# A deformable-convolution block: the gathered cells hold bilinear coefficients, made on VectorE, and ScalarE leaves the sampling

## The chip, the core and the metric

The kernel runs on one core of a Trainium2 chip. The metric is the device time of one execution in microseconds (us); before the change the median of three runs is 2737.15 us (2737.09 to 2738.84). TensorE (PE), VectorE (DVE), ScalarE (ACT), GpSimd (POOL) and SyncE (SP) run their own instruction streams and meet at semaphores.

## The reference

The input `x` has 4 images of 128 channels by 80x80 pixels, in float32. In short:

```
out_normal = conv3x3(x, w_normal)
offset     = concat(conv3x3(x, w_offx), conv3x3(x, w_offy))      # 18 channels: dy, dx of 9 taps
out_x, out_y = deform_conv(x, offset, w_dx), deform_conv(x, offset, w_dy)
out = relu(bn1(conv3x3(concat(out_normal, out_x, out_y), w_fusion)))   # 384 -> 128 channels
out = relu(bn2(conv3x3(out, w_conv2)) + x)

# deform_conv: for each pixel and tap (k) the position is (y + ky - 1 + dy, x + kx - 1 + dx),
# y0, x0 = its floors, ty, tx = what is left; outside the image a corner counts as zero:
s = (1-ty)(1-tx) x[y0,x0] + (1-ty)tx x[y0,x0+1] + ty(1-tx) x[y0+1,x0] + ty tx x[y0+1,x0+1]
result = sum over taps and channels of w[:, :, k] * s
```

Both deformable convolutions use the same samples `s`.

## The kernel before

**Tiling.** Each image is cut into 10 strips of 8 rows, 640 pixels, so there are 40 strips (`NS`) and 44 steps (`STEPS`); a step works on several strips at different stages. A strip has 9 taps, and the pixels of a tap are 5 tiles of 128 pixels (`TILES`). So a strip needs 45 gathers (`PER`), each of 128 cells, one per partition. A counter `T` numbers the taps of all strips, 360 in all.

**The cell table.** In device memory lies `cell_table`, one row of 2 KB per padded pixel: the 128 channels of its four neighbours (two of the upper row, two of the lower). SP builds it by DMAs from memory to memory (`fill`, L250 to L255): the first image's part whole, ahead of all else but the first loads, and the others in 27 parts of 768 rows, one per step.

**A tap's samples.** POOL issues an indirect DMA per tile (L318) into one of 15 cell slots; it waits until the slot's last reader is through (`mixed_done`) and until PE has come within five taps (`pace`). ACT then scales the upper pair (`upper`, L525, recorded at L495), DVE adds the lower pair (L700), giving `mixed`; ACT scales the left half (`left`, L533, recorded at L495), DVE adds the right half (L706), giving `samp`, pixels by channels. PE turns the five tiles to channels by pixels (`turn_samples`, L395); ACT copies the result rounded to `samp_hi` (L494), DVE subtracts to get `samp_lo` (L659), and PE multiplies both with the weights of the two deformable convolutions (`deform_tap`, lines L363, L366 and L369 of `three`, three matmuls per product). Between these PE works off slices of the other convolutions, by the table `SLICES`: C (second convolution), O (offsets), F (fusion) and N (normal).

**Order.** Each engine's program is written out in order, tap by tap. In step i, tap k, with T = 9i + k, PE turns the samples of T+1, then does its slices, then the products of T. ACT does `left` of T+2, `samp_hi` of T+1, `upper` of T+3. DVE does both its adds of T+2 (`sample`), then `samp_lo` of T+1. At a strip's end ACT and DVE empty the four accumulators (`feat<-acc`), and DVE works out the offsets' floors, fractions and row numbers (`indices`, L676 to L693). SP's program in a step is: load the strip after next (L248), load the residual (L286), fill a table part (L255), store an output strip after waiting for ACT (L294). The weights come in four chunks, split into a rounded and a remaining part by ACT and DVE (`w_hi` at L494, `w_lo` at L659).

Of the kernel before, what the change touches and what calls it, by code (L numbers as in the profile page):

```python
# [7 lines left out]
F32 = mybir.dt.float32  # L8
# [7 lines left out]
TAPS = 9  # L16
# [17 lines left out]
PART = 768  # L34
PARTS = CELLS // PART
FLAT = B * CELLS + 2 * PART
CELL = 4 * C
# [11 lines left out]
GSLOTS = 15  # L49
PACE_LAG = 5 * TILES  # L50
# [45 lines left out]
class Flags:  # L96


    def __init__(self, i=None, table=True):
# [17 lines left out]
        self.table = table if mid else i < (B - 1) * PARTS  # L117
# [17 lines left out]
def deform_block(nc, x, xflat, xpix, weights, bn, const, out):  # L135
    ctx = ExitStack()
    with ctx:
# [5 lines left out]

        table = nc.dram_tensor("cell_table", (B * CELLS, CELL), F32).ap()

# [35 lines left out]
        mixed = sb("mixed", [128, 2, TILES, 2 * C])  # L181
        samp = sb("samp", [128, 2, TILES, C])
# [20 lines left out]
        first_table, table_part = sem("first_table"), sem("table_part")  # L203
# [4 lines left out]
        slot_taken = sem("slot_taken")  # L208
# [33 lines left out]
        def _(eng):  # L242
# [7 lines left out]
            def fill(first, n, sem_):  # L250

                for row in range(2):
                    src = xpix[bass.ds(first + row * PITCH, n), :]
                    pairs = bass.AP(tensor=src.tensor, offset=src.offset, ap=[[C, n], [1, 2 * C]])
                    eng.dma_start(table[bass.ds(first, n), row * 2 * C:(row + 1) * 2 * C], pairs).then_inc(sem_, 16)  # L255
# [9 lines left out]
            fill(0, CELLS, first_table)  # L265
            load_weights(1)
            load_x(1)

            def step(i, par, fl):
                if isinstance(i, int) and i == 0:  # L270
                    eng.wait_ge(samp_done, PER // 3)
                if fl.load:
                    load_x(i + 2)
                if isinstance(i, int) and i == 1:
                    eng.wait_ge(w_lo_done, 2)
                    load_weights(2)
                    eng.wait_ge(w_lo_done, 3)
                    load_weights(3)
# [20 lines left out]
            eng.wait_ge(table_part, 32 * (B - 1) * PARTS)  # L299
# [4 lines left out]
        @block.gpsimd  # L304
        def _(eng):
            eng.memset(feat[:].bitcast(F32), 0.0).then_inc(zeroed, 1)
            eng.memset(mid[:].bitcast(F32), 0.0).then_inc(zeroed, 1)

            def gather(c, par, b):
                at_least(eng, idx_ready, c + 1)  # L310
                for q in range(PER):
                    k, j, g = q // TILES, q % TILES, q % GSLOTS
                    at_least(eng, mixed_done, PER * c + q - GSLOTS + 1)
                    at_least(eng, pace, PER * c + q - PACE_LAG + 1)
                    if not isinstance(c, int):

                        eng.sem_inc(slot_taken, 1)
                    eng.indirect_dma_start(  # L318
                        out=cells[:, g, :], out_offset=None, in_=table[0:(b + 1) * CELLS, :],
                        in_offset=bass.IndirectOffsetOnAxis(ap=index[:, par, j, k:k + 1], axis=0),  # L320
                    ).then_inc(cells_in[g], 16)


            eng.wait_ge(w_hi_done, 1)
            eng.wait_ge(w_lo_done, 1)
            for b in range(B):

                if b == 0:
                    eng.wait_ge(first_table, 32)
                else:  # L330
                    eng.wait_ge(table_part, 32 * PARTS * b)
                for c in range(b * STRIPS, (b + 1) * STRIPS):
                    gather(c, c % 2, b)
# [5 lines left out]
        def _(eng):  # L339
# [50 lines left out]
            def turn_samples(T, tp):  # L390

                at_least(eng, samp_done, TILES * T + TILES)
                at_least(eng, samp_lo_done, T)
                for j in range(TILES):
                    ins = eng.transpose(turned[:, j * 128:(j + 1) * 128], samp[:, tp, j, :], ident)  # L395
                ins.then_inc(samp_turned, 1)
# [20 lines left out]
            turn_samples(0, 0)  # L417

            def step(i, par, fl):
                early = isinstance(i, int) and i < 4  # L420
                for k in range(TAPS):
# [5 lines left out]
                    if fl.strip and (k < TAPS - 1 or fl.nxt):  # L427
                        turn_samples(T + 1, 1 - tp)
# [62 lines left out]
        def _(eng):  # L491
# [27 lines left out]
            def upper(T, c, k, par, tp):  # L519

                at_least(eng, samp_done, TILES * (T - 1))
                for j in range(TILES):
                    g, n = (k * TILES + j) % GSLOTS, (k * TILES + j) // GSLOTS + 1
                    at_least(eng, cells_in[g], (PER // GSLOTS * 16) * c + 16 * n)
                    copy(mixed[:, tp, j], cells[:, g, 0:2 * C], scale=wgt[:, par, 0, 0, j, k:k + 1])\  # L525
                        .then_inc(upper_done, 1)

            def left(T, k, par, tp):

                at_least(eng, samp_turned, T - 1)  # L530
                for j in range(TILES):
                    at_least(eng, mixed_done, TILES * T + j + 1)
                    copy(samp[:, tp, j], mixed[:, tp, j, 0:C], scale=wgt[:, par, 0, 1, j, k:k + 1]).then_inc(left_done, 1)  # L533
# [19 lines left out]
            upper(0, 0, 0, 0, 0)  # L553
            left(0, 0, 0, 0)
            x_high(1, 1)
            upper(1, 0, 1, 0, 1)
            samples_high(0, 0)
            left(1, 1, 0, 1)
            upper(2, 0, 2, 0, 0)
# [3 lines left out]
            def step(i, par, fl):  # L563
                for k in range(TAPS):
                    T = i * TAPS + k
                    tp = (par + k) % 2
                    if fl.strip and k < TAPS - 2:
                        left(T + 2, k + 2, par, tp)
                    elif fl.strip and fl.nxt:
                        left(T + 2, k + 2 - TAPS, 1 - par, tp)  # L570
# [5 lines left out]
                    if fl.strip and k < TAPS - 3:  # L576
                        upper(T + 3, i, k + 3, par, 1 - tp)
                    elif fl.strip and fl.nxt:
                        upper(T + 3, i + 1, k + 3 - TAPS, 1 - par, 1 - tp)
# [76 lines left out]
        def _(eng):  # L656
# [39 lines left out]
            def sample(T, k, par, tp):  # L696

                for j in range(TILES):
                    at_least(eng, upper_done, TILES * T + j + 1)
                    eng.scalar_tensor_tensor(  # L700
                        out=mixed[:, tp, j], in0=cells[:, (k * TILES + j) % GSLOTS, 2 * C:4 * C],
                        scalar=wgt[:, par, 1, 0, j, k:k + 1], in1=mixed[:, tp, j], op0=ALU.mult, op1=ALU.add,
                    ).then_inc(mixed_done, 1)
                for j in range(TILES):
                    at_least(eng, left_done, TILES * T + j + 1)
                    eng.scalar_tensor_tensor(  # L706
                        out=samp[:, tp, j], in0=mixed[:, tp, j, C:2 * C],
                        scalar=wgt[:, par, 1, 1, j, k:k + 1], in1=samp[:, tp, j], op0=ALU.mult, op1=ALU.add,
                    ).then_inc(samp_done, 1)
# [47 lines left out]
            sample(0, 0, 0, 0)  # L757
            x_low(1, 1)
            sample(1, 1, 0, 1)
            samples_low(0, 0)  # L760

            def step(i, par, fl):
                for k in range(TAPS):
# [3 lines left out]
                    if fl.strip and k < TAPS - 2:  # L767
                        sample(T + 2, k + 2, par, tp)
                    elif fl.strip and fl.nxt:
                        sample(T + 2, k + 2 - TAPS, 1 - par, tp)  # L770
# [95 lines left out]
```

## Time and profile before

| what | before |
|---|---|
| median of 3 runs | 2737.15 us |
| profiled execution: span, which is all that is shown of its time | 2989.8 us |
| PE busy, share of the span | 2685.1 us, 90% |
| ACT busy | 2004.2 us, 67% |
| POOL busy | 1870.2 us, 63% |
| DVE busy | 1849.5 us, 62% |
| bytes moved by DMA | 579.32 MB |
| mean granted TensorE clock | 0.983 |

The profiled execution is 253 us longer than the median of the runs; the profile does not say where these lie. "Busy" adds up the time that an engine's instructions cover. "Idle before" is time in which an engine did nothing ahead of an instruction, put down to what ended last before it; "issue" means that the profile shows nothing that it waited for. PE's matmuls overlap by construction, so a PE that is busy is not PE at its peak.

### The profile page before, as it was taken

To read this page: it belongs to the slowest core of one execution; us is meant where nothing else is said; L and a number is where in the kernel's file an instruction comes from. 1 tells how busy PE (TensorE), PEld (TensorE's weight loads), DVE (VectorE), ACT (ScalarE), POOL (GpSimd) and SP (SyncE) were. 2 spreads that over 40 slices of the span, in tenths; PEclk is the share of its full clock that TensorE was granted. 3 is DMA by queue.
4 is the path that set the end of the run, shared out by engine and by line. 5 is a ranking of instruction groups with operands and counts; after the bars stand their busy time and mean duration, and the time that the engine had idled before them with its cause. 6 is when DMAs were issued, how large, how long until landed. Compare 5 with 4: busy or idle time off the path is not lost.

```text
span 2989.8 us, 51480 instructions
## 1 busy us (share of the span) xinstructions
PE 2685.1 (90%) x17840; PEld 2612.5 (87%) x17840; DVE 1849.5 (62%) x4940; ACT 2004.2 (67%) x4925; POOL 1870.2 (63%) x1806
## 2 busy tenths in 40 slices
PE   1558899998999999999999999999999999999999
PEld 1458889998999998999899999999999999999999
DVE  3566666666666666666666666666666666666640
ACT  2566677776767676777677677776676776767741
POOL 3666666666666666666666666666666666666620
PEclk9789999999999999999999999999999999999999
DMA  9676667666666666666666767766666666666620
GB/s 278 202 231 193 206 200 220 202 208 198 205 205 201 198 208 199 201 206 205 204 204 203 215 209 219 215 181 186 183 186 183 181 182 186 186 182 185 179 90 23
DMA packets 218596, 579.32 MB, mean 194 GB/s; under 512 B 31840, under 2 KB 87264, under 8 KB 217952
## 3 DMA queue, kind: packets, MB, share of 16 engines
q0 software_dynamic: 144000, 471.97, 53.7%
q1 hardware_dynamic: 74336, 104.06, 10.5%
q8 instruction: 141, 2.31, 0.3%
q14 instruction: 119, 0.97, 0.1%
HBM read 562.80 MB, written 69.73 MB: 212 GB/s over the span
## 4 chain that ended last, share of the span: by engine, by line
PE 61%; ACT 13%; DVE 9%; issue 8%; another core or an unknown queue 7%; DMA 2%; POOL 1%; ACTq 0%; SPq 0%; POOLq 0%
PE work L363 13%; PE work L369 13%; PE work L366 13%; ACT mixed L495 5%; PE turned L395 5%; PE acc L369 5%; PE acc L366 5%; PE acc L363 5%; ACT samp L495 3%; DVE mixed L700 3%; PE work L348 2%; DVE feat L659 2%; DMA cell_table<-in_xpix 2%; DVE samp L706 2%
## 5 line engine op out<-in xcount | busy, mean ns | idle before, releaser
L318 POOL DMA_INDIRECT cells<-cell_table,index x1800 | 1859.0, 1033 | 1002.6 <-issue 390.4
L495 ACT ACTIVATE mixed<-cells,wgt 128x256 f32<-128x256 f32 x1800 | 758.0, 498 | 29.7 <-DMA cells<-cell_table,index 20.8
L495 ACT ACTIVATE samp<-mixed,wgt 128x128 f32<-128x128 f32 x1800 | 623.1, 396 | 205.6 <-issue 103.6
L700 DVE SCALAR_TENSOR_TENSOR mixed<-cells,wgt,mixed 128x256 f32<-128x256 f32 x1800 | 744.8, 478 | 21.8 <-ACT mixed L495 16.5
L363 PE MATMUL work<-feat,w_hi 128*128 128x320 f32 x2160 | 694.0, 321 | 13.7 <-issue 10.0
L369 PE MATMUL work<-feat,w_lo 128*128 128x320 f32 x2160 | 678.1, 314 | 10.9 <-issue 10.4
L366 PE MATMUL work<-feat,w_hi 128*128 128x320 f32 x2160 | 677.2, 314 | 7.4 <-issue 7.1
L706 DVE SCALAR_TENSOR_TENSOR samp<-mixed,wgt,samp 128x128 f32<-128x128 f32 x1800 | 512.0, 346 | 62.0 <-ACT samp L495 34.3
L659 DVE TENSOR_TENSOR samp_lo<-turned,samp_hi 128x640 fp32r<-128x640 f32 x360 | 295.8, 822 | 393.0 <-ACT samp_hi L494 329.2
L494 ACT ACTIVATE samp_hi<-turned 128x640 fp32r<-128x640 f32 x360 | 250.9, 697 | 374.3 <-remote 265.1
L363 PE MATMUL acc<-samp_hi,w_hi 128*128 128x320 f32 x1440 | 451.0, 313 | 11.9 <-issue 7.0
L366 PE MATMUL acc<-samp_lo,w_hi 128*128 128x320 f32 x1440 | 449.1, 312 | 12.7 <-issue 12.6
L369 PE MATMUL acc<-samp_hi,w_lo 128*128 128x320 f32 x1440 | 448.8, 312 | 8.5 <-issue 8.4
L363 PEld LDWEIGHTS work<-feat,w_hi 128*128 128x128 f32 x2160 | 409.3, 189 | 21.8 <-issue 21.5
L369 PEld LDWEIGHTS work<-feat,w_lo 128*128 128x128 f32 x2160 | 408.9, 189 | 14.2 <-issue 13.8
L366 PEld LDWEIGHTS work<-feat,w_hi 128*128 128x128 f32 x2160 | 409.5, 190 | 10.1 <-issue 10.1
L395 PE MATMUL turned<-cst,samp 128*128 128x128 f32 x1800 | 268.3, 279 | 165.9 <-DVE samp_lo L659 68.1
L395 PEld LDWEIGHTS turned<-cst,samp 128*128 128x128 f32 x1800 | 217.3, 143 | 190.9 <-issue 153.4
L369 PEld LDWEIGHTS acc<-samp_hi,w_lo 128*128 128x128 f32 x1440 | 273.5, 190 | 16.4 <-issue 16.3
L363 PEld LDWEIGHTS acc<-samp_hi,w_hi 128*128 128x128 f32 x1440 | 274.7, 191 | 13.9 <-DVE feat L659 7.7
L366 PEld LDWEIGHTS acc<-samp_lo,w_hi 128*128 128x128 f32 x1440 | 273.8, 190 | 14.0 <-issue 13.6
L363 PE MATMUL work<-mid,w_hi 128*128 128x320 f32 x720 | 233.5, 324 | 6.6 <-issue 6.5
(70 smaller groups left out, 3199.4 us busy)
## 6 DMA issues: line engine op xcount, KB each, us to landing
cell_table<-in_xpix SPq DMA_DIRECT2D x54, 768.0 KB
cells<-cell_table,index POOLq DMA_INDIRECT x1800
x_raw<-in_xflat SPq DMA_DIRECT2D x40, 410.0 KB
cell_table<-in_xpix SPq DMA_DIRECT2D x2, 6912.0 KB, 38.3
late<-in_x SPq DMA_DIRECT2D x40, 320.0 KB
out<-late SPq DMA_DIRECT2D x40, 320.0 KB
late<-in_weights SPq DMA_DIRECT2D x3, 1152.0 KB, 32.5
cells<-in_weights SPq DMA_DIRECT2D x1, 657.0 KB, 4.1
```

Source lines behind the costliest of these rows:

```text
L318: eng.indirect_dma_start(out=cells[:, g, :], out_offset=None, in_=table[0:(b + 1) * CELLS, :], in_offset=bass.IndirectOffsetOnAxis(ap=inde ...
L348: ins = eng.matmul(work[half][:, 0:HR * PITCH], w_off[:, ky, w].rearrange("p g n -> p (g n)"), part[:, par, rows, :], start=(n == 0), stop ...
L363: ins = eng.matmul(dst, taps_hi[:, w], hi, start=start, stop=False, skip_group_check=True)
L366: ins = eng.matmul(dst, taps_hi[:, w], lo, start=False, stop=False, skip_group_check=True)
L369: return eng.matmul(dst, w_lo[:, w], hi, start=False, stop=stop, skip_group_check=True)
L395: ins = eng.transpose(turned[:, j * 128:(j + 1) * 128], samp[:, tp, j, :], ident)
L494: return eng.activation(dst, src, ACT.Copy)
L495: return eng.activation(dst, src, ACT.Copy, scale=scale)
L659: return eng.tensor_tensor(dst, src, hi.bitcast(F32), ALU.subtract)
L700: eng.scalar_tensor_tensor(out=mixed[:, tp, j], in0=cells[:, (k * TILES + j) % GSLOTS, 2 * C:4 * C], scalar=wgt[:, par, 1, 0, j, k:k + 1], ...
L706: eng.scalar_tensor_tensor(out=samp[:, tp, j], in0=mixed[:, tp, j, C:2 * C], scalar=wgt[:, par, 1, 1, j, k:k + 1], in1=samp[:, tp, j], op0 ...
```

## The change

The host now lays out `corners`, a table of the four neighbours of every padded pixel, in place of the table that was filled on the device. From it 72 parts of 384 rows are loaded to on-chip memory, turned by DVE into coefficients, and stored to `coef_table`: the cell then holds a, b-a, c-a and (d-c)-(b-a). A sample is then (c0 + ty*c2) + tx*(c1 + ty*c3): one multiply-add of 256 wide and one of 128 wide, both on DVE. The first five strips (`RAW`) still gather from `corners` and keep the four operations of before. There are 12 cell slots in place of 15, `mixed` has three buffers in place of two and receives the result of the second operation as well, the pace lag is 6 taps in place of 5, and `samp_done` counts taps in place of tiles. ACT's `upper` runs one tap earlier, DVE's first operation runs a tap ahead of its second. SP stores and loads the parts behind the output's store, and loads the last weight chunk behind them.

```diff
-GSLOTS = 15
-PACE_LAG = 5 * TILES
+GSLOTS = 12
+PACE_LAG = 6 * TILES
+MIXED = 3
+LOT = 3
+PART = 128 * LOT
+RAW = 5
+PARTS_AT = [5, 5, 4, 4] + [4, 4, 4, 3, 3] + 18 * [2]
...
+        n = PARTS_AT[i] if i < len(PARTS_AT) else 0
+        self.parts = {j * TAPS // n: FIRST_PART[i] + j for j in range(n)}
...
+            def load_part(p):
+                at_least(eng, part_out, 16 * p)
+                eng.dma_start(coef[...], part_rows(corners, p)).then_inc(part_in, 16)
+            def store_part(p):
+                at_least(eng, part_done, 2 * p + 2)
+                eng.dma_start(part_rows(table, p), coef[...]).then_inc(part_out, 16)
...
-            fill(0, CELLS, first_table)
             load_weights(1)
             load_x(1)
+            load_part(0)
...
-                if fl.table:
-                    at_least(eng, table_part, 32 * i)
-                    fill(CELLS + i * PART, PART, table_part)
                 if fl.second:
                     s = i - 4
                     at_least(eng, out_ready, 2 * s + 2)
                     eng.dma_start(out[:, bass.ds(s * PIX, PIX)], resid[:, par]).then_inc(out_stored[par], 16)
+                for p in fl.parts.values():
+                    store_part(p)
+                    if p + 1 < B * PARTS:
+                        load_part(p + 1)
+                if isinstance(i, int) and i == 1:
+                    eng.wait_ge(w_lo_done, 3)
+                    load_weights(3)
...
+            for c in range(NS):
+                b = c // STRIPS
+                if c < RAW:
+                    gather(c, c % 2, corners[0:CELLS, :])
+                    continue
+                if c == RAW or c % STRIPS == 0:
+                    eng.wait_ge(part_out, 16 * PARTS * (b + 1))
+                gather(c, c % 2, table[0:(b + 1) * CELLS, :])
...
+            def upper(T):
+                if T >= TAPS * RAW:
+                    return
...
+            def weigh(T):
+                if T >= TAPS * RAW:
+                    return
...
+            def rows_mixed(T):
+                k, par, raw = T % TAPS, T // TAPS % 2, T < TAPS * RAW
+                if not raw:
+                    at_least(eng, samp_turned, T - MIXED + 1)
+                for j in range(TILES):
+                    n = T * TILES + j
+                    cell, into = cells[:, n % GSLOTS, :], mixed[:, T % MIXED, j]
+                    if raw:
+                        at_least(eng, upper_done, n + 1)
+                    else:
+                        at_least(eng, cells_in[n % GSLOTS], 16 * (n // GSLOTS) + 16)
+                    eng.scalar_tensor_tensor(
+                        out=into, in0=cell[:, 2 * C:4 * C], scalar=wgt[:, par, 1, 0, j, k:k + 1],
+                        in1=into if raw else cell[:, 0:2 * C], op0=ALU.mult, op1=ALU.add,
+                    ).then_inc(mixed_done, 1)
+            def sampled(T):
...
+                for j in range(TILES):
+                    ins = eng.scalar_tensor_tensor(
+                        out=mixed[:, buf, j, 0:C], in0=mixed[:, buf, j, C:2 * C],
+                        scalar=wgt[:, par, 1, 1, j, k:k + 1], in1=mixed[:, buf, j, 0:C], op0=ALU.mult, op1=ALU.add)
+                ins.then_inc(samp_done, 1)
+            def coefficients(p):
+                at_least(eng, part_in, 16 * p + 16)
+                eng.tensor_tensor(coef[:, :, :, 1], coef[:, :, :, 1], coef[:, :, :, 0], ALU.subtract).then_inc(part_done, 1)
+                at_least(eng, part_done, 2 * p + 1)
+                eng.tensor_tensor(coef[:, :, 1], coef[:, :, 1], coef[:, :, 0], ALU.subtract).then_inc(part_done, 1)
...
-                    if fl.strip and k < TAPS - 2:
-                        sample(T + 2, k + 2, par, tp)
...
+                    sampled(T + 2)
                     if fl.strip and (k < TAPS - 1 or fl.nxt):
                         samples_low(T + 1, 1 - tp)
+                    rows_mixed(T + 3)
+                    if k in fl.parts:
+                        coefficients(fl.parts[k])
```

## Rows read from the trace of the kernel before

**Rows 1.** Busy time of each engine over the span, from the page.

```profile
PE 2685.1 (90%) x17840; PEld 2612.5 (87%) x17840; DVE 1849.5 (62%) x4940; ACT 2004.2 (67%) x4925; POOL 1870.2 (63%) x1806
```

**Rows 2.** Busy time by stretch: window, length, engines, clock, DMA share, GB/s.

```profile
66.00:132.00 66.00, 32.40 (x182) 31.05 (x181) 41.33 (x113) 41.60 (x107) 46.51 (x46) 0.82 0.68 211
132.00:200.00 68.00, 42.23 (x233) 39.36 (x231) 44.23 (x120) 44.31 (x113) 47.26 (x46) 0.80 0.66 198
500.00:2700.00 2200.00, 2069.95 (x13906) 2018.01 (x13905) 1429.89 (x3832) 1553.10 (x3831) 1443.94 (x1404) 1.00 0.66 198
```

**Rows 3.** Timeline of the first 66 us: start, length, engine, line, [idle before <-releaser].

```profile
2.58 19.68 SPq L255 DMA_DIRECT2D cell_table<-in_xpix  x2
22.30 23.11 SPq L259 DMA_DIRECT2D late<-in_weights  x1
23.66 0.25 DVE L693 TENSOR_SCALAR index<-above,cst 128x45 int32<-128x45 f32 x1
52.95 1.09 POOL L318 DMA_INDIRECT cells<-cell_table,index  x1 [41.15 <-DMA cell_table<-in_xpix]
57.02 2.56 DVE L659 TENSOR_TENSOR w_lo<-late,w_hi 128x2304 fp32r<-128x2304 f32 x1 [33.11 <-ACT w_hi L494]
58.09 2.31 POOL L318 DMA_INDIRECT cells<-cell_table,index  x1 [0.30 <-issue]
65.12 1.30 PE L395 MATMUL turned<-cst,samp 128*128 128x128 f32 x5 [48.03 <-DVE samp L706]
```

**Rows 4.** What PE waited for ahead of the turning (L395), 500 to 2700 us.

```profile
  issue: 24.8, 31
  DVE samp_lo L659: 21.3, 15
  DVE samp L706: 6.3, 3
```

**Rows 5.** Timeline of one strip's end, DVE, ACT and PE.

```profile
1505.85 1.68 DVE L659 TENSOR_TENSOR feat<-acc,feat 128x320 fp32r<-128x320 f32 x4
1507.45 2.06 DVE L700 SCALAR_TENSOR_TENSOR mixed<-cells,wgt,mixed 128x256 f32<-128x256 f32 x5
1509.42 1.40 DVE L706 SCALAR_TENSOR_TENSOR samp<-mixed,wgt,samp 128x128 f32<-128x128 f32 x5
1510.74 0.82 DVE L659 TENSOR_TENSOR samp_lo<-turned,samp_hi 128x640 fp32r<-128x640 f32 x1
...
1510.15 0.31 PE L369 MATMUL acc<-samp_hi,w_lo 128*128 128x320 f32 x1
1511.70 0.74 PE L395 MATMUL turned<-cst,samp 128*128 128x128 f32 x5 [1.24 <-DVE samp_lo L659]
```

**Rows 6.** DMA queues (packets, MB, share of 16 engines' span), and issues by line to landing.

```profile
q0 software_dynamic: 144000, 471.97, 53.7%
q1 hardware_dynamic: 74336, 104.06, 10.5%
late<-in_weights SPq DMA_DIRECT2D x3, 1152.0 KB, 32.5
cells<-in_weights SPq DMA_DIRECT2D x1, 657.0 KB, 4.1
```

**Rows 7.** Groups of instructions from 500 to 2700 us: count, busy, mean ns, idle before.

```profile
L318 POOL DMA_INDIRECT cells<-cell_table,index x1404 | 1444.2, 1029 | 758.4 <-issue 300.3 <-PE work L363 169.6 <-DVE mixed L700 119.7
L495 ACT ACTIVATE mixed<-cells,wgt 128x256 f32<-128x256 f32 x1400 | 587.1, 498 | 0.0
L495 ACT ACTIVATE samp<-mixed,wgt 128x128 f32<-128x128 f32 x1400 | 486.6, 396 | 163.3 <-issue 87.6 <-DVE mixed L700 66.8 <-PE turned L395 2.0
```

**Rows 8.** DVE's own subtractions with both inputs on chip, whole run.

```profile
L659 DVE TENSOR_TENSOR x_lo<-x_raw,x_hi 128x820 fp32r<-128x820 f32 x40 | 40.6, 1014 | 11.2 <-issue 6.3 <-ACT x_hi L494 4.9
```

**Rows 9.** What SP waited for at the output's store, whole run: us, times, longest.

```profile
SPq L294 <- ACT late L631: 522.8, 27, 66.2
```

More of the change, by code:

```diff
@@ L33 @@
 CELLS = 6912
-PART = 768
+FLAT = B * CELLS + 2 * 768
+CELL = 4 * C
+LOT = 3
+PART = 128 * LOT
 PARTS = CELLS // PART
-FLAT = B * CELLS + 2 * PART
-CELL = 4 * C
+RAW = 5
+PARTS_AT = [5, 5, 4, 4] + [4, 4, 4, 3, 3] + 18 * [2]
+assert sum(PARTS_AT) == B * PARTS
+FIRST_PART = [sum(PARTS_AT[:i]) for i in range(len(PARTS_AT) + 1)]
 assert (H + 2 * LEAD - 1) * PITCH + 1 <= CELLS and CELLS % PART == 0
@@ L96, with __init__ @@
 class Flags:
-    def __init__(self, i=None, table=True):
+    def __init__(self, i=None):
         mid = i is None
@@ L132, in at_least, with deform_block @@
     eng.wait_ge(sem, value)
-def deform_block(nc, x, xflat, xpix, weights, bn, const, out):
+def deform_block(nc, x, xflat, corners, weights, bn, const, out):
     ctx = ExitStack()
@@ L180, in deform_block @@
         cells = sb("cells", [128, GSLOTS, CELL])
-        mixed = sb("mixed", [128, 2, TILES, 2 * C])
-        samp = sb("samp", [128, 2, TILES, C])
+        coef = sb("coef", [128, LOT, 2, 2, C])
+        mixed = sb("mixed", [128, MIXED, TILES, 2 * C])
         samp_hi = sb("samp_hi", [128, 2, PIX], F32R)
@@ L248, in load_x, with part_rows @@
                 eng.dma_start(x_raw[:], xflat[:, bass.ds(start, SLOT)]).then_inc(x_in, 16)
[L250 to L255, printed above, removed]
+            def part_rows(of, p):
+                return of[p * PART:(p + 1) * PART, :].rearrange("(q n) c -> q (n c)", n=LOT)
+            def load_part(p):
+                at_least(eng, part_out, 16 * p)
+                eng.dma_start(coef[:, :, :, :, :].rearrange("q n a b c -> q (n a b c)"),
+                              part_rows(corners, p)).then_inc(part_in, 16)
+            def store_part(p):
+                at_least(eng, part_done, 2 * p + 2)
+                eng.dma_start(part_rows(table, p),
+                              coef[:, :, :, :, :].rearrange("q n a b c -> q (n a b c)")).then_inc(part_out, 16)
             def load_weights(n):
@@ L307, in _, with gather @@
             eng.memset(mid[:].bitcast(F32), 0.0).then_inc(zeroed, 1)
-            def gather(c, par, b):
+            def gather(c, par, source):
                 at_least(eng, idx_ready, c + 1)
                 for q in range(PER):
[L312 to L317, printed above, removed]
+                    k, j, n = q // TILES, q % TILES, PER * c + q
+                    at_least(eng, mixed_done, n - GSLOTS + 1)
+                    at_least(eng, pace, n - PACE_LAG + 1)
                     eng.indirect_dma_start(
-                        out=cells[:, g, :], out_offset=None, in_=table[0:(b + 1) * CELLS, :],
+                        out=cells[:, n % GSLOTS, :], out_offset=None, in_=source,
                         in_offset=bass.IndirectOffsetOnAxis(ap=index[:, par, j, k:k + 1], axis=0),
-                    ).then_inc(cells_in[g], 16)
+                    ).then_inc(cells_in[n % GSLOTS], 16)
             eng.wait_ge(w_hi_done, 1)
             eng.wait_ge(w_lo_done, 1)
[L326 to L333, printed above, removed]
+            for c in range(NS):
[6 more added lines that the diff above has]
+                gather(c, c % 2, table[0:(b + 1) * CELLS, :])
         @block.tensor
@@ L566, in step @@
                     tp = (par + k) % 2
-                    if fl.strip and k < TAPS - 2:
-                        left(T + 2, k + 2, par, tp)
-                    elif fl.strip and fl.nxt:
-                        left(T + 2, k + 2 - TAPS, 1 - par, tp)
+                    weigh(T + 2)
                     if fl.strip and (k < TAPS - 1 or fl.nxt):
@@ L574, in step @@
                         weights_high(fl.weights[k])
[L576 to L579, printed above, removed]
+                    upper(T + 4)
                     if k == fl.turn and fl.nxt:
@@ L700, in sample @@
                     eng.scalar_tensor_tensor(
-                        out=mixed[:, tp, j], in0=cells[:, (k * TILES + j) % GSLOTS, 2 * C:4 * C],
-                        scalar=wgt[:, par, 1, 0, j, k:k + 1], in1=mixed[:, tp, j], op0=ALU.mult, op1=ALU.add,
+                        out=into, in0=cell[:, 2 * C:4 * C], scalar=wgt[:, par, 1, 0, j, k:k + 1],
+                        in1=into if raw else cell[:, 0:2 * C], op0=ALU.mult, op1=ALU.add,
                     ).then_inc(mixed_done, 1)
-                for j in range(TILES):
[L705 to L709, printed above, removed]
+            def sampled(T):
+                if T >= TAPS * NS:
+                    return
+                k, par, buf = T % TAPS, T // TAPS % 2, T % MIXED
+                if T < TAPS * RAW:
+                    at_least(eng, left_done, TILES * T + TILES)
+                else:
+                    at_least(eng, mixed_done, TILES * T + TILES)
+                for j in range(TILES):
+                    ins = eng.scalar_tensor_tensor(
+                        out=mixed[:, buf, j, 0:C], in0=mixed[:, buf, j, C:2 * C],
+                        scalar=wgt[:, par, 1, 1, j, k:k + 1], in1=mixed[:, buf, j, 0:C], op0=ALU.mult, op1=ALU.add)
+                ins.then_inc(samp_done, 1)
```

68 lines of the change are left out of this document (33 added, 35 removed).

## Prediction

> **What bounds the kernel now.** I read the page's busy times first, then the stretches, then the start's timeline, then the waits of PE in the steady part.
>
> Over the span PE is busy 90% and no other engine over 67% [rows 1]. From 500 to 2700 us there are 1404 gathers, 45 to a strip, so 31.2 strips of 70.5 us; in each PE is busy 66.3 us, ACT 49.8, POOL 46.3, DVE 45.8, at a granted clock of 1.00 [rows 2]. This part is PE's. The first two strips, 66 and 68 us long, are not: PE is busy only 32.4 and 42.2 us of them, and no engine over 47.3; they run through the chain gather, ACT, DVE, ACT, DVE, PE [rows 2]. Before them stands a start in which nothing samples: the row numbers are ready at 23.91, but the first gather goes out at 52.95, ended by the DMA that builds the first table, and PE turns the first samples at 65.12 [rows 3].
>
> So there are two places to gain: the start, and whatever PE still waits for in the steady part. The latter is small. Ahead of the turning of samples PE stood idle 24.8 + 21.3 + 6.3 = 52.4 us in 31.2 strips, 1.7 us a strip [rows 4]; releasers are DVE's two last products, or none that is shown. One instance reads: PE's last product starts at 1510.15, its turning at 1511.70, with 1.24 us of idle released by `samp_lo`; DVE before that had no pause from 1505.85 on: accumulators, `mixed`, `samp`, `samp_lo` [rows 5].
>
> **The change, part by part.** The sums go by the profiled execution. The page gives its span, 2989.8 us, and nothing around it; the runs' median is 2737.15, a factor of 0.9155. Where the 253 us lie can't be read, so terms set by DMA and DVE are carried over whole, and a steady strip is put at 70.5 x 0.9155 = 64.5 us, an estimate.
>
> *Start.* The first table's fill goes, and the second weight chunk no longer stands behind its issue (2.58 + 19.68 us, then the chunk's issue of 23.11 us) [rows 3]. The first gather then needs only the row numbers: 52.95 - 23.91 = 29 us earlier. The chunk is needed at the first product. A chunk of 657 KB landed in 4.1 us, three of 1152 KB with a median of 32.5, behind other transfers [rows 6]; I take the first row's side, since only small loads are ahead of it. What is late next is DVE's `w_lo` of that chunk, 2.56 us, which will fall on the first gathers: one gather beside it took 2.31 us, the first one 1.09 [rows 3]. I take -27 us; bounds -29 and, if the chunk needs 32.5 us from an issue at about 3, -17 (35.5 against 52.95).
>
> *ACT's two operations* go for 35 of 40 strips. They cover (587.1 + 486.6)/31.2 = 34.4 us of ACT per strip [rows 7], but PE never shows ACT as what it waits for at the turning [rows 4]. By itself nothing.
>
> *DVE's order.* DVE's two multiply-adds stay as many and as wide. What changes is that the wide one of a tap is done a step earlier. At a strip's end `samp` and `samp_lo` then follow the accumulators at once, and the five wide ones, 2.06 us, leave the stretch that PE waits for [rows 5]. That would close a gap of up to 2.06 us; the gap is 1.7. Lower bound 0: the gap's releaser may become ACT's `samp_hi` or the gathers. In the faster run PE reaches this point earlier, so the gap may be wider, but POOL is closer to its own limit: 45 x (1.029 [rows 7] + 0.30 of issue [rows 3]) = 59.8 us of 64.5. Between 0 and 2.06 I take 1.0 us, times 35 strips: -35, bounds 0 and -72.
>
> *Coefficients.* Each part adds two subtractions over 768 elements. The nearest row is 820 elements in 1.014 us [rows 8], so 0.95 us each, 1.9 a part. From step 9 on there are two parts a step, 3.8 us on a DVE that is busy 45.8 of 70.5 [rows 2]: hidden behind PE. If that cover were gone it would be 18 x 3.8 = 68 us. In the first five strips 22 parts cost 42 us of DVE, and there PE does not cover them; but DVE is idle 24 us in each of the first two [rows 2], so little shows.
>
> *The part's wait.* `coefficients` waits on DVE, in order, for the load, which waits on SP for the store of the part before. Behind it stand the emptying of the convolutions, `indices`, and the next tap's `samp`, and on these PE. One transfer of 786 KB is bounded by 4.1 and 32.5 us [rows 6]; I take about 5, near the 657 KB row, so 10 for store and load. In steps 0 and 1 the second part comes one tap after the first, some 7.5 us, so DVE stands still about 2.5 us; elsewhere parts are two to four taps apart. From step 4 on SP must first see ACT finish the output strip, a wait that already held it 522.8 us in 27 cases [rows 9]; the store of a step's first part then goes out about two taps into the step, and with four parts a step (steps 4 to 6) the second one waits some 5 us. Behind SP's queue nothing else is late: the next strip's load is needed a step later.
>
> *DMA.* The small queue moved 104.06 MB in 10.5% of the span, 314 us, or 3.0 us per MB [rows 6]. The fills' 56.6 MB (27,648 rows of 2 KB) become 113.2 (72 parts, in and out), so 171 us more, 6% on a share of 0.66 [rows 2]: hidden in the steady part. In the first two strips it adds up: 45 gathers at 0.537 x 2989.8/1800 = 0.89 us are 40.1; five parts of 1.57 MB, 23.6; input and a weight chunk, 1.6 MB, 4.8: 68.5 us against strips of 66 and 68. So the early strips become bound by DMA at about their present length.
>
> For the early strips together I take +12 us: 3 each for the first two by DMA, 2.5 each for their waits, and the rest for the steps with four parts. Bounds: -10 (the new order helps there too) and +35 (DVE's 42 us nearly whole).
>
> *Twelve slots and a lag of six taps.* POOL may now be 12 cells ahead of DVE's wide operation, which itself runs a tap earlier. With 15 slots POOL waited 119.7 us for `mixed`, 3.8 us a strip [rows 7], and PE did not notice. I cost it at nothing; without cover it is part of the second rival.
>
> Sum: 2737 - 27 + 12 - 35 = 2687.
>
> **The rivals.**
>
> *Only the start is gained.* The gap at the strip's end goes to another releaser, say the gathers. For it: 24.8 of the 52.4 us have none that is shown [rows 4]. Against it: DVE had no pause in the instance [rows 5]. 2737 - 27 + 12 = 2722.
>
> *GpSimd becomes the bound, slower.* Place: the spacing of gathers in the 35 later strips. A gather beside DVE's long subtraction took 2.31 us in place of about 1 [rows 3], so each of four coefficient instructions a strip may hold a gather for up to 0.95 us: 59.8 + 3.8 = 63.6. With the present wait for slots, 3.8 [rows 7], a strip takes 67.4. It decides from 64.5 on, and at its full price gives 35 x 2.9 = +102: 2737 - 15 + 102 = 2824. Against it: the mean gather is only 1.029 us beside all of DVE's present work [rows 7], and POOL now also waits for PE's pace, so part of its waits is spare.
> The Trainium skill (SBUF — State Buffer, Who interferes with whom) says that a DVE instruction with two inputs in on-chip memory contends with a GpSimd instruction that reads it, and one of them blocks. The row of 2.31 us agrees. By the rule taken alone all 144 new subtractions collide, and the sum would be this rival's.
>
> *Everything in the sampling path speeds up.* The gap closes by the full 2.06 us and the early strips gain what they lose: 2737 - 29 - 72 = 2636. For it: ACT drops out as a middleman whose products waited 66.8 us on `mixed` [rows 7]. Against it: POOL at 59.8.
>
> *The change does not do what it says* can't be: the code shows each operation.
>
> **How the numbers follow.** The forecast 0.50, only the start 0.22, all of the path 0.17, GpSimd as the bound 0.11. A measurement of this kernel tells 0.2%, 5.5 us, from no change. The forecast and the third case are faster; of the second, with bounds of the early strips, about three quarters are faster and the rest the same; GpSimd's is slower. So faster 0.83, same 0.06, slower 0.11. The range reaches from the third case, 2635, to 2738, most of the way to the second with the early strips at their dear end (2722 + 23 = 2745); GpSimd's case is left out.
>
> **What would show it.** The first gather at about 24 us and PE's first turning near 38; no DVE idle over 5 us that a part's load ended, except in steps 0, 1 and 4 to 6; idle before L395 under 0.7 us a strip; DVE near 49.6 us of busy time a strip, ACT near 15.4; POOL's gathers at a mean below 1.06 us. The prediction is wrong if steady strips in the profile are no shorter than 70.5 us, if the early strips are longer by over 35 us together, or if POOL's waits for `mixed` grow and PE's idle time with them.

## The result: slower, by the early strips

The changed kernel takes 2766.8 us (2760.6 to 2768.0) against 2738.0 before, a ratio of 1.0097 (95% interval 1.0082 to 1.0111). The prediction was 2687 and faster. The profiled execution's span is 2766.2 us, as long as its runs; that of the kernel before was 253 us longer than its runs, so a second profile of it was taken in the experiments (span 2735.2 us), and the comparisons below are with that one.

The page's busy times of the changed kernel, which answer to [rows 1]:

```profile
PE 2623.4 (95%) x17840; PEld 2610.6 (94%) x17840; DVE 1966.9 (71%) x5084; ACT 868.8 (31%) x1775; POOL 1852.4 (67%) x1806
```

ACT fell from 2004 to 869 us of busy time, and nothing came of it. The stretches say where the time is. First the changed kernel's, answering to [rows 2]: window, length, then busy time of PE, PEld, DVE, ACT, POOL, granted clock, DMA share, GB/s. The first five rows are strips 0 to 4.

```profile
38.00:114.00 76.00, 38.19 (x190) 35.77 (x191) 49.74 (x125) 46.17 (x114) 56.14 (x53) 0.68 0.83 269
114.00:190.00 76.00, 43.02 (x228) 40.85 (x226) 51.52 (x128) 45.87 (x112) 47.77 (x45) 0.73 0.79 276
190.00:261.00 71.00, 61.16 (x391) 59.82 (x392) 58.07 (x134) 50.54 (x122) 50.42 (x44) 0.93 0.83 282
261.00:335.00 74.00, 62.64 (x399) 60.62 (x399) 51.93 (x131) 48.28 (x121) 49.24 (x46) 0.93 0.78 258
335.00:414.00 79.00, 70.06 (x451) 68.81 (x450) 55.48 (x140) 45.43 (x109) 48.87 (x45) 0.94 0.75 249
600.00:1800.00 1200.00, 1200.00 (x8302) 1198.87 (x8301) 919.42 (x2367) 324.23 (x619) 858.20 (x840) 1.00 0.78 252
```

And the kernel before, in its second profile:

```profile
66.00:130.00 64.00, 35.35 (x188) 33.81 (x189) 43.04 (x116) 43.31 (x110) 49.67 (x48) 0.74 0.73 223
130.00:191.00 61.00, 41.93 (x227) 40.67 (x226) 43.63 (x118) 44.59 (x112) 47.34 (x45) 0.78 0.74 220
191.00:263.00 72.00, 59.85 (x401) 58.85 (x401) 49.87 (x125) 53.68 (x126) 55.43 (x49) 0.93 0.75 245
263.00:322.00 59.00, 56.35 (x389) 55.62 (x388) 43.63 (x120) 49.02 (x121) 45.50 (x44) 1.00 0.77 236
322.00:389.00 67.00, 65.88 (x454) 65.33 (x453) 47.31 (x127) 51.05 (x126) 51.89 (x50) 1.00 0.77 235
500.00:2500.00 2000.00, 2000.00 (x13838) 1998.14 (x13837) 1418.78 (x3818) 1542.64 (x3819) 1458.29 (x1397) 1.00 0.73 217
```

In both kernels PE is busy for the whole of the steady part, to the last digit. A strip there takes 64.4 or 64.5 us in each. From turning to turning the five early strips took 63.4, 61.7, 71.1, 59.7 and 66.9 us and take 75.1, 76.8, 71.0, 73.3 and 79.3; the windows above are these strips to within a microsecond. The outer bounds are PE's turnings of the first sample of strip 0 and of strip 5; here those of the changed kernel,

```profile
38.44 0.87 PE L408 MATMUL turned<-cst,mixed 128*128 128x128 f32 x3 [21.84 <-DVE mixed L739]
413.92 0.71 PE L408 MATMUL turned<-cst,mixed 128*128 128x128 f32 x5
```

and of the kernel before:

```profile
66.34 0.88 PE L395 MATMUL turned<-cst,samp 128*128 128x128 f32 x3 [49.65 <-DVE samp L706]
389.16 0.71 PE L395 MATMUL turned<-cst,samp 128*128 128x128 f32 x5
```

So sampling starts 27.9 us earlier, the early strips take 375.5 us in place of 322.8, 52.7 more, and strips 5 and 6 take 66.3 and 68.9, 6.3 over 64.45 each. That is -27.9 + 52.7 + 6.3 = +31.1, and the spans differ by 31.0. Nothing else moved.

PE's granted clock differs too: 0.93 and 0.94 in strips 3 and 4, a mean over its two levels (1.2 and 2.4 GHz), where it was 1.00, the higher level throughout. For the same 1659 matmuls PE is busy 275.1 us in the first five rows and was busy 259.4. PE also stands idle for longer in these strips; whether the lower clock adds to their length or only goes with it, no run here separates.

The start is as it was forecast: the first gather goes out as soon as the row numbers are there, and it runs beside the second weight chunk's subtraction. It takes 2.61 us and ends 0.97 us after that subtraction, where the next one takes 0.95; [rows 3] had shown the like.

```profile
23.17 0.25 DVE L707 TENSOR_SCALAR index<-above,cst 128x45 int32<-128x45 f32 x1
23.45 2.56 DVE L673 TENSOR_TENSOR w_lo<-late,w_hi 128x2304 fp32r<-128x2304 f32 x1
24.37 2.61 POOL L330 DMA_INDIRECT cells<-in_corners,index  x1 [12.56 <-DVE index L707]
27.28 0.95 POOL L330 DMA_INDIRECT cells<-in_corners,index  x1 [0.30 <-issue]
```

What the early strips wait for, in the changed kernel from 38 to 414 us (us in total, times, longest):

```profile
ACT mixed L508 <- DMA cells<-in_corners,index: 105.9, 74, 5.7
DVE mixed L739 <- ACT mixed L508: 67.2, 28, 6.8
PE turned L408 <- DVE samp_lo L673: 65.5, 23, 10.7
POOL cells L330 <- DVE mixed L724: 65.1, 58, 6.5
DVE coef L747 <- DMA coef<-in_corners: 16.2, 3, 7.6
```

These waits read as a circle: ACT waits for cells, DVE for ACT, and POOL for DVE to free a slot, so that the cells come later; in the second profile of before, POOL's waits of this kind in strips 0 to 4 are 17.4 us. The DMAs of the changed kernel, answering to [rows 6]: the small queue went from 11.2% in the second profile of before to 15.8%, and a gather of the early strips lands in 5.4 us, a later one in 3.9.

```profile
q0 software_dynamic: 144000, 471.97, 56.5%
q1 hardware_dynamic: 38880, 160.69, 15.8%
coef<-in_corners SPq DMA_DIRECT2D x72, 768.0 KB, 6.8
cells<-coef_table,index POOLq DMA_INDIRECT x1575, 3.9
cells<-in_corners,index POOLq DMA_INDIRECT x225, 5.4
```

### The profile page after: what moved, and what is told of

It reads as the page before. It is cut to its first block, busy times and chain, and to the rows that moved or that the text cites. A ratio compares the mean times of both kernels' runs of the same rounds, so it can differ in the third digit from the quotient of the medians.

```text
span 2766.2 us, 48198 instructions
## 1 busy us (share of the span) xinstructions
PE 2623.4 (95%) x17840; PEld 2610.6 (94%) x17840; DVE 1966.9 (71%) x5084; ACT 868.8 (31%) x1775; POOL 1852.4 (67%) x1806
## 3 DMA queue, kind: packets, MB, share of 16 engines
q1 hardware_dynamic: 38880, 160.69, 15.8%
## 4 chain that ended last, share of the span: by engine, by line
PE 86%; DMA 5%; DVE 5%; issue 2%; ACT 1%; POOL 1%; SPq 0%; POOLq 0%; ACTq 0%; DVEq 0%
PE work L376 18%; PE work L382 18%; PE work L379 18%; PE acc L376 7%; PE acc L379 7%; PE acc L382 7%; PE turned L408 6%; PE work L361 3%; DMA cells<-in_corners,index 3%; DVE mixed L739 1%; DMA coef<-in_corners 1%; DVE mixed L724 1%; DMA coef_table<-coef 1%; POOL cells L330 1%; ACT mixed L508 1%
## 5 line engine op out<-in xcount | busy, mean ns | idle before, releaser
L330 POOL DMA_INDIRECT cells<-coef_table,index x1575 | 1597.8, 1014 | 661.0 <-issue 278.5
L724 DVE SCALAR_TENSOR_TENSOR mixed<-cells,wgt 128x256 f32<-128x256 f32 x1575 | 650.7, 480 | 0.5 <-DMA cells<-coef_table,index 0.5
L739 DVE SCALAR_TENSOR_TENSOR mixed<-mixed,wgt 128x128 f32<-128x128 f32 x1800 | 503.9, 347 | 73.3 <-ACT mixed L508 68.1
L408 PE MATMUL turned<-cst,mixed 128*128 128x128 f32 x1800 | 263.0, 278 | 103.9 <-DVE samp_lo L673 69.8
L330 POOL DMA_INDIRECT cells<-in_corners,index x225 | 243.3, 1082 | 132.7 <-DVE mixed L724 64.2
L408 PEld LDWEIGHTS turned<-cst,mixed 128*128 128x128 f32 x1800 | 221.1, 143 | 114.0 <-DVE mixed L739 77.8
L376 PE MATMUL work<-x_hi,w_hi 128*128 128x320 f32 x720 | 232.4, 323 | 9.3 <-ACT late L613 9.3
```

Source lines behind the costliest of these rows:

```text
L330: eng.indirect_dma_start(out=cells[:, n % GSLOTS, :], out_offset=None, in_=source, in_offset=bass.IndirectOffsetOnAxis(ap=index[:, par, j, ...
L376: ins = eng.matmul(dst, taps_hi[:, w], hi, start=start, stop=False, skip_group_check=True)
L408: ins = eng.transpose(turned[:, j * 128:(j + 1) * 128], mixed[:, T % MIXED, j, 0:C], ident)
L724: eng.scalar_tensor_tensor(out=into, in0=cell[:, 2 * C:4 * C], scalar=wgt[:, par, 1, 0, j, k:k + 1], in1=into if raw else cell[:, 0:2 * C] ...
L739: ins = eng.scalar_tensor_tensor(out=mixed[:, buf, j, 0:C], in0=mixed[:, buf, j, C:2 * C], scalar=wgt[:, par, 1, 1, j, k:k + 1], in1=mixed ...
```

## The experiments

Two theories stood at the outset: the parts (their traffic, subtractions and waits) lengthen the early strips, or the twelve slots do.

**The kernel before again** (no edit).

> The kernel before, unchanged, for a second profile: its first profiled execution (2989.8 us) was 253 us longer than its timed runs, while that of the changed kernel (2766.2) is as long as its timed runs. If the 253 us are stalls of that one execution, this span is near 2736 us, and strips 5 to 38 take about 64.4 us each, as in the changed kernel: then PE alone sets the steady part in both and nothing was to be gained there. The rival: the steady strips of before are longer (65 us or more) and the change did shorten them.

Measured: 2737.05 us, span 2735.2. Strips 5 to 38 take 64.4 or 64.5 us. Its groups from 500 to 2500 us show no idle time before any matmul; here the first product, and the turning whose waits made up [rows 4]:

```profile
L363 PE MATMUL work<-feat,w_hi 128*128 128x320 f32 x1678 | 536.8, 320 | 0.0
L395 PE MATMUL turned<-cst,samp 128*128 128x128 f32 x1395 | 197.8, 272 | 0.0
```

The same two groups and window in the first profile had this:

```profile
L363 PE MATMUL work<-feat,w_hi 128*128 128x320 f32 x1512 | 485.0, 321 | 9.5 <-issue 7.7 <-ACT off_c L494 1.8
L395 PE MATMUL turned<-cst,samp 128*128 128x128 f32 x1279 | 186.5, 275 | 48.5 <-issue 21.7 <-DVE samp_lo L659 21.3 <-DVE samp L706 4.2
```

The gap that the change was to close belonged to that one execution.

**No parts, twelve slots** (label noparts12).

```diff
-        self.parts = {j * TAPS // n: FIRST_PART[i] + j for j in range(n)}
+        self.parts = {}
...
-            load_part(0)
...
-                gather(c, c % 2, table[0:(b + 1) * CELLS, :])
+                gather(c, c % 2, corners[0:(b + 1) * CELLS, :])
```

> The changed kernel without any coefficient part: no loads, no subtractions, no stores; strips 5 and on gather from the corners and treat them as coefficients, so that part of the computation is left out. Theory 1, the parts' traffic, subtractions and waits lengthen the early strips: strips 0 to 6 fall from 510 us to about 460, time about 2715. Theory 2, the twelve slots lengthen them (POOL waited 65 us for DVE's first operation there): strips 0 to 6 stay above 490, time above 2745.

**The same, fifteen slots** (noparts15: `GSLOTS = 15`).

> The same without parts, with 15 slots in place of 12 (the room of the coefficients' buffer is free). Theory 1: within 5 us of the 12-slot one. Theory 2: 25 us or more faster than it, near 2705.

**The kernel before, gathering from the host's corners** (b_corners).

```diff
-            fill(0, CELLS, first_table)
...
-                    fill(CELLS + i * PART, PART, table_part)
...
-                        out=cells[:, g, :], out_offset=None, in_=table[0:(b + 1) * CELLS, :],
+                        out=cells[:, g, :], out_offset=None, in_=xpix[0:(b + 1) * CELLS, :],
...
+    xpix = np.concatenate([xpix[o:o + B * CELLS] for o in (0, 1, PITCH, PITCH + 1)], axis=1)
```

> The kernel before with all gathers from the corners that the host lays out: no table is filled on the device, all else as before (15 slots, ACT's two operations). If the start's 27 us are a gain of their own, 2737 - 27 = 2710, and some 5 to 10 us less if the fills held up the early gathers, 2702. If the early strips' chain absorbs it, 2730 or more.

Measured, with all later runs; "start" is PE's first turning, "strips 0 to 4" from there to the first turning of strip 5, both from one profile each; the ratio is to the kernel before on the same chip.

| kernel | median us | ratio, 95% | start | strips 0 to 4 |
|---|---|---|---|---|
| before (second profile) | 2737.05, one run | | 66.3 | 322.8 |
| after | 2766.80 | 1.0097 (1.0082 to 1.0111) | 38.4 | 375.5 |
| noparts12 | 2723.61 | 0.9946 (0.9930 to 0.9963) | 38.1 | 336.2 |
| noparts15 | 2714.63 | 0.9915 (0.9899 to 0.9932) | 37.7 | 326.1 |
| b_corners | 2705.02 | 0.9879 (0.9863 to 0.9896) | 36.7 | 320.1 |
| parts_thin | 2734.05 | 0.9986 (0.9976 to 0.9996) | 38.0 | 345.4 |
| parts_dve | 2737.54 | 0.9993 (0.9984 to 1.0003) | 37.7 | 347.5 |
| parts_dve2 | 2781.82 | 1.0161 (1.0143 to 1.0180) | 38.4 | 371.7 |
| raw20 | 2799.81 | 1.0221 (1.0204 to 1.0238) | 37.9 | 337.9 |
| raw0_15 | 2697.56 | 0.9850 (0.9833 to 0.9866) | 36.6 | 315.7 |
| noparts10 | 2752.43 | 1.0059 (1.0041 to 1.0077) | 37.3 | 365.4 |
| after10 | 2800.96 | 1.0241 (1.0222 to 1.0259) | 38.3 | 403.0 |
| raw40_15 | 2767.51 | 1.0106 (1.0089 to 1.0122) | 38.5 | 328.4 |

The parts cost 2766.8 - 2723.6 = 43 us; both theories hold a share, the parts' being the larger: three slots are worth 9.0 us, between what the two expected. The remaining step from noparts15 to b_corners, 9.6, is all else in the change that bears on the first five strips: the order of the four operations, three buffers of `mixed`, waits counted by taps, the pace lag and the last weight chunk's place, which no run takes apart. So, taken in this order, the change is made up of -33.1 (before to b_corners), +9.6, +9.0 and +43.2, which is its +28.8 to 0.1. b_corners computes the whole reference and is faster than both kernels, by 1.2% and 2.2%.

**Which of the part's costs.** parts_thin keeps the transfers and the waits, parts_dve the subtractions alone, with all gathers from the corners.

```diff
# parts_thin (its partner the same way)
-eng.tensor_tensor(coef[:, :, :, 1], coef[:, :, :, 1], coef[:, :, :, 0], ALU.subtract)
+eng.tensor_tensor(coef[:, 0, 0, 1, 0:1], coef[:, 0, 0, 1, 0:1], coef[:, 0, 0, 0, 0:1], ALU.subtract)
# parts_dve
-                at_least(eng, part_in, 16 * p + 16)
...
-                for p in fl.parts.values():
-                    store_part(p)
```

> The changed kernel with its part loads, stores and waits, but each subtraction cut to one column (most of the coefficients' arithmetic is left out). The parts cost 45 us in all (changed kernel 2767, without parts 2724). Theory 1, their DMA and the waits for it cost: time stays at 2750 or above. Theory 2, DVE's 2 x 0.96 us a part cost (42 us in the first five strips): time falls to 2735 or below.

> The subtractions alone at full width, on a buffer that is never loaded or stored; all gathers from the corners, so the coefficients are left out of the result. Theory 1 (DMA): near 2730, 5 us over the kernel without parts. Theory 2 (DVE's work): 2745 or more. If both terms are of one size, thin parts and this one lie 15 to 30 us over 2724 each.

Measured 10 and 14 us over noparts12. Neither theory alone: both terms are smaller than expected, and they add up to 24, not 43. The gathers of parts_thin land in 5.0 us, in noparts12 in 3.7, so slower landing by itself costs no more than these 10. The other 19 are only in part accounted for. In strips 5 and 6, which take 64.4 or 64.5 us in parts_thin and in parts_dve, the full change takes 6.3 us more. And DVE waits longer for a part's load: 16.2 us in the first five strips (the last row of the waits above), and from 38 to 549 us, to the end of strip 6,

```profile
DVE coef L747 <- DMA coef<-in_corners: 38.9, 7, 9.2
```

where parts_thin has in its first five strips:

```profile
DVE coef L747 <- DMA coef<-in_corners: 10.3, 3, 4.4
```

One of the seven, in strip 5, on DVE and then on SP (start, length, instruction, idle before):

```profile
436.75 2.10 DVE L724 SCALAR_TENSOR_TENSOR mixed<-cells,wgt 128x256 f32<-128x256 f32 x5
446.94 0.96 DVE L747 TENSOR_TENSOR coef<-coef 128x768 f32<-128x768 f32 x1 [8.09 <-DMA coef<-in_corners]
...
434.07 0.34 SPq L302 DMA_DIRECT2D out<-late  x1
434.46 0.43 SPq L268 DMA_DIRECT2D coef_table<-coef  x1
440.45 0.33 SPq L263 DMA_DIRECT2D coef<-in_corners  x1
```

The coefficients had been ready since 428.5, but their store stood behind the output's, which SP issued at 434.07; store 6.0 us, load 6.5, and DVE idle for 8.09.

**Does idle time take up the first cost?** parts_dve2 does every subtraction of parts_dve twice.

```diff
...
+                at_least(eng, part_done, 4 * p + 2)
+                eng.tensor_tensor(coef[:, :, :, 1], coef[:, :, :, 1], coef[:, :, :, 0], ALU.subtract).then_inc(part_done, 1)
+                at_least(eng, part_done, 4 * p + 3)
+                eng.tensor_tensor(coef[:, :, 1], coef[:, :, 1], coef[:, :, 0], ALU.subtract).then_inc(part_done, 1)
```

> The subtractions alone, no transfers, each part's two done twice (the coefficients are left out of the result). Once they cost 14 us over 2724, of 42 us of DVE in the first five strips. If idle time of DVE takes up the first ones and not the second, the second 42 us cost 25 or more: 2762 or above. If the cost is even, 14 more: 2751.

Measured 2781.8: the second helping costs 44 us. Some 27 of them lie in strips 5 to 26, which go from 64.45 us to 65.7; there the first helping had cost nothing. So where PE is the bound, idle time takes up the first helping and not all of the second. From 500 to 1700 us, parts_dve and then parts_dve2:

```profile
500.00:1700.00 1200.00, 1200.00 (x8303) 1198.89 (x8302) 920.04 (x2367) 324.98 (x619) 852.95 (x839) 1.00 0.68 201
500.00:1700.00 1200.00, 1187.25 (x8154) 1177.57 (x8153) 979.23 (x2417) 311.67 (x603) 881.07 (x825) 1.00 0.67 198
```

That leaves, by the medians, 17 us for the early strips, against 14 for the first helping. The two profiles say 24.2 and 11.3, but they are one execution each, the one 2.7 us over its kernel's median and the other 4.5 under it. So that the cost rises in the early strips is not shown, nor that a wait for a load uses up the same idle time as work does.

Nor need a subtraction cost by DVE's time alone. A gather issued during one is longer, as here in the changed kernel:

```profile
1013.01 0.97 DVE L747 TENSOR_TENSOR coef<-coef 128x768 f32<-128x768 f32 x1
1013.04 1.75 POOL L330 DMA_INDIRECT cells<-coef_table,index  x1 [0.30 <-PE acc L376]
1015.10 0.95 POOL L330 DMA_INDIRECT cells<-coef_table,index  x1 [0.30 <-PE work L376]
```

The gathers of the early strips with none, one and two helpings (noparts12, parts_dve, parts_dve2):

```profile
L327 POOL DMA_INDIRECT cells<-in_corners,index x236 | 242.3, 1027 | 94.6 <-issue 46.6 <-DVE mixed L719 34.7 <-PE acc L371 6.2
L324 POOL DMA_INDIRECT cells<-in_corners,index x235 | 255.4, 1087 | 91.5 <-issue 46.3 <-DVE mixed L716 29.6 <-PE acc L368 10.4
L324 POOL DMA_INDIRECT cells<-in_corners,index x233 | 272.9, 1171 | 101.0 <-DVE mixed L716 43.6 <-issue 42.7 <-PE acc L371 6.0
```

POOL's busy time grows by 13 and 17 us, about as much as the helpings cost there. Whether the subtractions lengthen the early strips by DVE's time or by the gathers that they hold up, no run here separates.

**Parts where PE covers them** (raw20): the first two images gathered from the corners by four operations, coefficients for the last two.

```diff
-RAW = 5
-PARTS_AT = [5, 5, 4, 4] + [4, 4, 4, 3, 3] + 18 * [2]
+RAW = 20
+P0 = 2 * PARTS
+PARTS_AT = 5 * [0] + 18 * [2]
...
```

> The same computation as the reference, with the first two images gathered from the corners by the four operations, and coefficients for the last two alone: 36 parts, two a step in steps 5 to 22, none in the early steps. If only parts in the early strips cost and PE covers them later, the time is that of the kernel without parts, 2724, within 5 us; if they cost wherever they stand, 22 us more (36 of 72 parts of 45 us).

Measured 2799.8: both expectations missed. Strips 0 to 4 are as without parts (337.9), but strips 5 to 19 take 68.6 to 72.5 us, and only from strip 20 on 64.4 or 64.5. The four operations, as the change orders them and with its slots and parts, do not keep up with PE.

**Two operations from the start** (raw0_15: `RAW = 0` in noparts15).

> No parts, 15 slots, and the two-operation path from the first strip on, on corners taken as coefficients (the computation of the coefficients is left out). It shows what taking ACT out of the sampling is worth where PE is not the bound. If the early strips hang on the hand-overs between ACT and DVE, strips 0 to 4 fall from 326 us to 300 or below, time 2690; if they hang on the gathers, 5 x 60 us and more, they stay near 320, time 2708 or above.

Measured 2697.6, between the two. Without ACT in the sampling the early strips take 315.7 us in place of 326.1 in the profiles, and the medians differ by 17 us. So taking ACT out is worth 10 to 17 us where PE is not the bound, if coefficients came for nothing.

**Fewer slots, with and without parts** (`GSLOTS = 10`).

> The changed kernel with 10 slots in place of 12. If the early strips run round a loop of slots (a gather's landing, ACT, DVE's first operation, the slot free again), longer with parts because gathers land in 5.4 us and not 3.7 and DVE does more, then two slots less cost more here than without parts: 20 us or more, 2787 or above. If slots and parts are separate costs, the same as without parts: 6 to 10 us, 2775.

> The kernel without parts (coefficients left out) with 10 slots. From 15 to 12 it lost 9 us, 3 a slot: 6 to 10 us more, 2732, if the loss is even; 15 or more, 2740, if the loop tightens.

Measured +34.2 and +28.8 us. The loss per slot rises, 3.0 us from 15 to 12 and 14.4 from 12 to 10, as a loop that tightens would give. That the loop is tighter with parts is not shown: 34 and 29 are within their intervals of each other.

**The new order in all strips** (raw40_15: `RAW = 40` in noparts15).

> The new order of the four operations (ACT's upper and DVE's first operation a tap earlier, three buffers) for all 40 strips, from the corners, with 15 slots and no parts: the same computation as the reference. With two of four images gathered raw, 12 slots and parts, strips 5 to 19 took 69 to 72 us. If the order of the four operations causes this, these strips take 67 or more here and the time is 2790 or above; if the slots and parts do, they take 64.4 and the time is that of the 15-slot kernel without parts, 2715.

Measured 2767.5: between the two again. Each steady strip takes 66.0 us, 1.6 over PE's own time, with 15 slots and no parts. PE's waits from 500 to 2500 us in this kernel, about 1 us a strip, name the place, above all DVE's emptying of the second convolution:

```profile
PE work L356 <- DVE late L836: 21.4, 30, 1.0
PE work L371 <- ACT off_c L502: 7.9, 30, 0.3
```

DVE in turn waited 391.6 us for ACT's scaling in that window. raw20's excess is 5.2 us a strip on average, so if costs added up, a third of it would be the order; how the rest splits between slots and parts was not tried.

## Why the prediction was wrong, step by step

- *Start: right.* Forecast -27, measured -27.9; the chunk landed in time, and the first gather took 2.61 us beside `w_lo`.
- *DVE's order, -35: there was nothing to gain.* The step read 1.7 us of idle a strip ahead of the turning [rows 4] and an instance of it [rows 5]. In the second profile PE has none there. The first execution was 253 us longer than the runs, which the prediction stated, and nearly half of the idle time it counted was released by "issue", that is, by nothing shown. The estimate of 64.5 us for a strip was right to 0.1; had the step asked how much PE itself needs of these 64.5, all of it, the term would have been nil. Its own rows said so: PE's 66.3 us of busy time a strip [rows 2] is already more than 64.5. Its own caution, that the gap may belong to another releaser, chose between causes and not whether there was a gap.
- *The early strips, +12: the term that was mis-sized.* Measured +52.7, with +6.3 in strips 5 and 6, so 59, above the bound of 35; the parts alone cost 43 of it. The pieces were priced sensibly: a subtraction 0.956 us for 0.95, a load 6.8 us to landing for about 5, DVE's waits in steps 0, 1 and 4 to 6 as named, though at 2.5 and 5 us where the longest were 7.6 and 9.2. What failed is the step from DVE's idle time to "so little shows": because DVE was idle 24 us in each of the first two strips, 42 us of subtractions were put at next to nothing. Alone they cost 14 us, the transfers with their waits 10, and both together 43. DVE's idle time there was not spare: 67.2 us of it went in waiting for ACT, which stood 105.9 us waiting for cells. Why the two together cost 19 us more than their sum is shown only in part (strips 5 and 6, longer waits for loads) and stays open.
- *Early strips bound by DMA: did not come.* The step set 68.5 us of DMA against strips of 66 and 68. The DMA share of the first two strips is 0.83 and 0.79 of 76 us, 63 and 60 us, and the strips are longer than that.
- *Twelve slots at nothing: wrong.* Three slots less cost 9.0 us, all in the early strips. The reasoning that PE did not notice POOL's waits came from the steady part, where PE covers them; in the early strips nothing does.
- *The new order in the first five strips:* the bound of -10 had the wrong sign. With three buffers and all else that goes with it, it costs 6 us in these strips by the profiles and 9.6 by the medians (noparts15 against b_corners); which part of it does so was not tried.
- *The slower rival, GpSimd as the bound: did not come, though its mechanism is there.* Steady gathers with the subtractions take 1.022 us on average, without them, in noparts12, 0.987: 1.6 us a strip where the rival took 3.8. The kernel before, 1.044 in the second profile, is no measure of it, since its operations on DVE are others. The collision that the Trainium skill states (SBUF — State Buffer, Who interferes with whom) is seen at the long subtraction of 2.56 us and at the short ones (1.75 us beside one of 0.97). But 45 gathers at 1.022 and 0.30 of issue are 59.5 us, still under PE's 64.4. The slower case that came was another: the early strips.
- *The rival that only the start is gained* was right on the steady part; it shared the +12, and so missed too.
- *The signs.* The first gather, the start, the idle time before the turning, DVE's 49.4 us a strip and the mean gather came out as the prediction had said, ACT at 17.4 us a strip for 15.4, and steady strips are shorter than 70.5 us. Those of the steady part could not tell a right prediction from a wrong one, because the kernel before, in a second profile, shows 64.4 us and no idle time as well. The signs that did tell were the early strips, longer by over 35 us, and there POOL's waits for `mixed`, 65.1 us for 17.4, with PE's idle time.

The rows for gathers, answering to [rows 7], from 500 to 1700 us of the changed kernel and of noparts12 and, in a fence of its own, from 500 to 2500 us of the second profile of before:

```profile
L330 POOL DMA_INDIRECT cells<-coef_table,index x837 | 855.8, 1022 | 344.2 <-issue 147.2 <-DVE mixed L724 121.0 <-PE work L376 44.4
L327 POOL DMA_INDIRECT cells<-in_corners,index x838 | 826.7, 987 | 373.6 <-DVE mixed L719 152.9 <-issue 149.2 <-PE work L371 44.2
L747 DVE TENSOR_TENSOR coef<-coef 128x768 f32<-128x768 f32 x41 | 39.2, 955 | 16.7 <-DMA coef<-in_corners 16.7
```

```profile
L318 POOL DMA_INDIRECT cells<-cell_table,index x1397 | 1458.6, 1044 | 541.8 <-issue 261.3 <-DVE mixed L700 196.4 <-PE work L363 72.0
```

## What to carry to other kernels

Before costing a change by a profile, hold its span against the runs: here it was 9% longer, its small gaps were not the kernel's, and a second profile was cheap. Where one engine has no idle time at all, relief of the others was worth nothing, so look for the part in which no engine is the bound. There, in this kernel, a loop of buffers and hand-overs set the pace: three slots less cost 9 us, and two costs of 10 and 14 us alone made 43 together. Idle time of an engine in such a loop is not free room, and small costs cannot be held against it one by one. What a collision costs is read from two kernels that differ in it alone. The gain here could be had alone: laying the corners out on the host, with nothing else changed, gives 2705.0 us.

## What was not expected of the hardware

One profiled execution of the kernel before showed idle time ahead of matmuls, much of it released by "issue", and 70.5 us a strip in place of 64.4, with the same granted clock of 1.00; another execution of the same program showed none. What caused it stays open.
